# A two-layer block on one core: PV of a slot moved behind both its pairs of scores and of maxima, and the first batch's routing and expert tiles moved behind the first scores

## The reference

```python
x = L0_attn_x                                  # (4, 1024, 128) f32
xn = layernorm(x)
x = x + attn0(xn) + moe(xn)                    # layer 0
xn = layernorm(x)
x = x + attn1(xn) + fp4_ffn(xn)                # layer 1
```

## Time and profile before

| | us |
|---|---|
| median of 3 runs | 1758.02 |
| lowest and highest | 1752.01, 1764.23 |
| the profiled execution | 1775.41 |
| its span, first to last instruction | 1773.3 |
| PE, DVE, ACT, POOL busy | 1532.3, 1350.8, 1156.3, 580.5 |

### The profile page before, as it was taken

How to read it: one execution, slowest core, us unless ns; L and a number is a source line. 1 busy time by engine, 2 the same in 40 slices (tenths; PEclk the granted TensorE clock), 3 DMA queues, 4 the chain that set the end, 5 groups by cost and what they waited for, 6 DMA issues and landing times.

```text
span 1773.3 us, 35212 instructions
## 1 busy us (share of the span) xinstructions
PE 1532.3 (86%) x10813; PEld 643.4 (36%) x10813; DVE 1350.8 (76%) x3482; ACT 1156.3 (65%) x2716; POOL 580.5 (33%) x530
## 2 busy tenths in 40 slices
PE   3389969888999999778999999688999978989996
PEld 1233423333334444223333454233444424334332
DVE  6698858759998677659898866577888867888881
ACT  2067758747888566447887755455888864766665
POOL 3302120111454233241544414311141464553530
PEclk8599989979999899869999989888999987999999
DMA  7423622211612113321711112512353200310000
GB/s 228 110 83 95 163 60 69 63 42 42 179 46 58 31 47 120 89 72 44 188 45 34 57 31 77 164 44 63 96 163 102 62 26 2 101 44 2 14 2 13
DMA packets 162918, 131.84 MB, mean 74 GB/s; under 512 B 30825, under 2 KB 130098, under 8 KB 162738
## 3 DMA queue, kind: packets, MB, share of 16 engines
q1 hardware_dynamic: 158642, 121.19, 25.1%
q0 software_dynamic: 4096, 8.40, 1.6%
HBM read 88.50 MB, written 40.50 MB: 73 GB/s over the span
## 4 chain that ended last, share of the span: by engine, by line
PE 58%; DVE 20%; issue 7%; ACT 6%; another core or an unknown queue 4%; POOL 4%; SPq 1%; DMA 1%; DVEq 0%; ACTq 0%; POOLq 0%
PE ring L493 38%; PE pO L493 16%; DVE mparts L1108 10%; ACT PR L771 4%; PE ring L496 4%; DVE junk L1112 1%; DVE xn L1175 1%; POOL rows_in L695 1%; DVE hs L1398 1%; DVE xr L1288 1%; DVE hs L1397 1%; DVE stats L1158 1%; ACT hid L834 1%; POOL rstd L665 1%
## 5 line engine op out<-in xcount | busy, mean ns | idle before, releaser
L771 ACT ACTIVATE PR<-ring 128x512 f32<-128x512 f32 (+3 forms) x1792 | 882.9, 557 | 351.8 <-PE ring L493 292.9
L1108 DVE TENSOR_REDUCE mparts<-ring 128x1 f32<-128x512 f32 x1280 | 811.0, 683 | 211.0 <-PE ring L493 152.9
L493 PE MATMUL pO<-PR,VX 128*9 128x512 f32 (+3 forms) x3584 | 449.0, 575 | 7.6 <-ACT PR L771 6.9
L493 PE MATMUL ring<-KX,QX 48*128 48x512 bf16 (+3 forms) x1792 | 341.4, 376 | 93.1 <-ACT PR L771 60.6
L493 PE MATMUL ring<-QX,KX 50*128 50x512 bf16 (+3 forms) x1792 | 339.6, 375 | 59.4 <-DVE mparts L1108 35.6
L493 PEld LDWEIGHTS ring<-QX,KX 50*128 50x128 bf16 x1792 | 89.7, 93 | 519.2 <-DVE mparts L1108 244.4
L1112 DVE CUSTOM_DVE_ANT_0 junk<-ring,diag 128x384 bf16<-128x384 f32 (+3 forms) x512 | 227.8, 487 | 65.3 <-PE ring L493 55.2
L721 POOL TENSOR_SCALAR bq<-bq 128x352 f32<-128x352 f32 (+1 forms) x40 | 47.1, 1177 | 449.9 <-ACT bq L871 439.2
L493 PEld LDWEIGHTS ring<-KX,QX 48*128 48x128 bf16 x1792 | 96.3, 95 | 187.6 <-issue 77.1
L834 ACT ACTIVATE hid<-ring,b1r 128x128 f32<-128x128 f32 x368 | 105.2, 369 | 52.6 <-PE ring L493 47.4
L710 POOL DMA_INDIRECT ra<-rows_out,at x64 | 61.2, 956 | 234.4 <-DMA rows_out<-yb 141.6
(11 more groups left out here) (156 smaller groups left out, 1507.6 us busy)
## 6 DMA issues: line engine op xcount, KB each, us to landing
scratch<-parts SPq DMA_DIRECT2D x96, 256.0 KB, 3.7
w1r<-in_w SPq DMA_DIRECT2D x92, 256.0 KB
w2r<-in_w SPq DMA_DIRECT2D x92, 256.0 KB
QX<-scratch SPq DMA_DIRECT2D x128, 96.0 KB, 3.2
KX<-scratch SPq DMA_DIRECT2D x64, 192.0 KB, 3.8
xg<-rows_in SPq DMA_DIRECT2D x92, 64.0 KB
rows_out<-yb SPq DMA_DIRECT2D x92, 64.0 KB
QX<-mT SPq DMA_DIRECT2D x256, 2.0 KB
```

Of the source, the lines that this page charges most:

```text
L493: return nc.tensor.matmul(dst, lhsT, rhs, start=start, stop=stop, **kw)
L771: nc.scalar.activation(PR[:, n % 2, HALF * j + off:HALF * j + HALF], ring[plan.bank("E", k)][:, off:HALF], ACT.Exp, scale=SCALE).then_inc( ...
L1108: v.tensor_reduce(dst, src[:, 0:w], axis=X, op=ALU.max).then_inc(s_mr, 1)
```

## The change

It has five parts.

1. PE's order in a slot: first scores, first maxima, second scores, second maxima, then PV, then the pieces. ACT's four exponentials of a step stand together, and the copy of `pO` and the `hi` and `mid` copies follow them.
2. The first batch's gate logits, routing, scatters and tiles go behind the first scores: `lg` at slot 40, the scatters in slots 50 to 57, the tiles from slot 60 to 111 (before: 9, 19 to 26, and 29 to 102). The preparation of batch 1 moves from slots 42 to 61 to slots 59 to 70. The gathers of batch 0 move from slots 104 to 111 to slots 113 to 120. The turned fp4 weights (`wT`) go from slots 15 to 17 to 33 to 35.
3. Preparations may put three pieces in a slot (`most`).
4. The first four projection halves have four pairs of buffers, two of them lent by `hid` and `oT`, and their remainder on DVE is one step later in the slot. ACT waits for their readers before it writes `oT` and `hid` for the first time.
5. POOL clears the second operand set after the first four `lo` parts in place of after the first `rstd`, and the first loads wait for five clears in place of seven.

```diff
@@ -71,13 +71,17 @@
-                done = self.finish(p)
-                self.tiles(p)
+                self.finish(p)
+                if p:
+                    self.tiles(p)
...
-                    self.prepare(p + 1, self.start[p] + (2 if p else 4), self.projected[p - 1] + 1 if p else 0)
+                    self.prepare(p + 1, self.start[p] + 2 if p else self.gated[p] + T + 2,
+                                 self.projected[p - 1] + 1 if p else 0)
+                    if p == 0:
+                        self.tiles(p)
@@ -96,8 +100,8 @@
-    def put(self, i, event):
-        while len(self.slot(i)["xs"]) >= 2:
+    def put(self, i, event, most=2):
+        while len(self.slot(i)["xs"]) >= most:
@@ -146,7 +150,7 @@
-        to = {0: self.start[1] + 2, 1: self.start[3] - 4, 2: self.start[5] - 4, 3: self.start[6] - 8}[b]
+        to = {0: self.start[1] + 6, 1: self.start[3] - 4, 2: self.start[5] - 4, 3: self.start[6] - 8}[b]
@@ -171,6 +175,7 @@
+        at = max(at, self.start[0] - 6)
@@ -184,22 +189,22 @@
-            i = self.put(i + 1, ("xT", p, h))
+            i = self.put(i + 1, ("xT", p, h), 3)
...
-                    i = self.put(i + 1, ("pj", p, q, h, "a"))
-                    i = self.put(i, ("pj", p, q, h, "b"))
+                    i = self.put(i + 1, ("pj", p, q, h, "a"), 3)
+                    i = self.put(i, ("pj", p, q, h, "b"), 3)
...
-                        self.slot(i + 1)["small"][0].append(("rem", p, q, h))
+                        self.slot(i + 1)["small"][3].append(("rem", p, q, h))
...
-                    i = self.put(i + 1, ("pj", p, q, h, ""))
+                    i = self.put(i + 1, ("pj", p, q, h, ""), 3)
@@ -207,7 +212,8 @@
-            j = self.put(i + 1, ("lg", p))
...
+            j = self.put(i + 1 if p else self.start[0] + 2, ("lg", p))
@@ -517,6 +523,14 @@
+        def sums(n):
...
+            return hid[n % 2][:, :] if n in (2, 3) else ra[:, n % 2, :]
...
+        def left(n):
...
+            return oT[n % 2][:, :] if n in (2, 3) else rb[:, n % 2, :]
@@ -562,7 +576,7 @@
                                 sp.wait_ge(s_scr[q], 96 * (p + 1))
-                                sp.wait_ge(s_pre, 7)
+                                sp.wait_ge(s_pre, 7 if p else 5)
                                 if p >= 2:
@@ -663,25 +677,25 @@
-                            if p == 0:
-                                clear(1)
...
-                            nc.gpsimd.tensor_tensor(ra[:, n % 2, :], ra[:, n % 2, :], rb[:, n % 2, :],
+                            nc.gpsimd.tensor_tensor(sums(n), sums(n), left(n),
...
-                            nc.gpsimd.tensor_tensor(rb[:, n % 2, :], ra[:, n % 2, :], parts[:, q, 0, half],
+                            nc.gpsimd.tensor_tensor(left(n), sums(n), parts[:, q, 0, half],
...
-                            nc.gpsimd.tensor_tensor(parts[:, q, 2, half], rb[:, n % 2, :], parts[:, q, 1, half],
+                            nc.gpsimd.tensor_tensor(parts[:, q, 2, half], left(n), parts[:, q, 1, half],
...
+                            if lows == 4:
+                                clear(1)
@@ -750,11 +764,11 @@
-                def exps(s, js):
+                def exps(s):
...
-                    if js[0] == 0 and plan.steps[s["step"]] == 0:
+                    if plan.steps[s["step"]] == 0:
...
@@ -773,10 +787,13 @@
-                    exps(s, (0, 1))
+                    exps(s)
...
+                        if k == 0:
...
+                            act.wait_ge(s_lo, 4)
@@ -788,11 +805,10 @@
-                            copy(parts[:, q, 0, half], ra[:, n % 2, :]).then_inc(s_hi, 1)
+                            copy(parts[:, q, 0, half], sums(n)).then_inc(s_hi, 1)
...
-                            copy(parts[:, q, 1, half], rb[:, n % 2, :]).then_inc(s_mid, 1)
-                    exps(s, (2, 3))
+                            copy(parts[:, q, 1, half], left(n)).then_inc(s_mid, 1)
@@ -808,8 +824,8 @@
-                            if p == 0:
-                                act.wait_ge(s_pre, 7)
+                            if p < 2:
+                                act.wait_ge(s_pre, (5, 7)[p])
@@ -828,6 +844,9 @@
+                            if N == 0:
...
+                                act.wait_ge(s_rem, 4)
...
@@ -927,8 +946,9 @@
-                    scores(s, 0)
-                    maxima(s, 0)
+                    for pair in range(2):
+                        scores(s, pair)
+                        maxima(s, pair)
@@ -948,8 +968,6 @@
-                    scores(s, 1)
-                    maxima(s, 1)
@@ -1198,7 +1216,7 @@
-                            dve.wait_ge(s_pre, 7)
+                            dve.wait_ge(s_pre, 3)
...
@@ -1356,15 +1374,15 @@
-                            if n >= 2:
+                            if n >= 4:
...
-                                ins = v.tensor_tensor(ra[:, n % 2, :], src[:, :], rc[:, half], ALU.mult)
+                                ins = v.tensor_tensor(sums(n), src[:, :], rc[:, half], ALU.mult)
...
-                                ins = v.tensor_tensor(rb[:, n % 2, :], src[:, :], rs[:, half], ALU.mult)
+                                ins = v.tensor_tensor(left(n), src[:, :], rs[:, half], ALU.mult)
...
-                                ins = v.tensor_tensor(rb[:, n % 2, :], src[:, :], parts[:, q, 0, half], ALU.subtract)
+                                ins = v.tensor_tensor(left(n), src[:, :], parts[:, q, 0, half], ALU.subtract)
```

More of the change, by code:

```diff
@@ L767, in exps @@
                         act.wait_ge(s_pv, n - 1)
-                    for j in js:
+                    for j in range(G):
                         k = 4 * n + j
@@ L862, in _ @@
                             act.wait_ge(s_rem, plan.parts0[p, q, h] + 1)
-                            copy(parts[:, q, 1, HALF * h:HALF * h + HALF], rb[:, n % 2, :]).then_inc(s_mid, 1)
+                            copy(parts[:, q, 1, HALF * h:HALF * h + HALF], left(n)).then_inc(s_mid, 1)
                         if e[0] == "gates":
@@ L1298, in small_step @@
                         dve.wait_ge(s_hi, n + 1)
-                        v.tensor_tensor(rb[:, n % 2, :], ra[:, n % 2, :], parts[:, q, 0, HALF * h:HALF * h + HALF],
+                        v.tensor_tensor(left(n), sums(n), parts[:, q, 0, HALF * h:HALF * h + HALF],
                                         ALU.subtract).then_inc(s_rem, 1)
@@ L1410, in _ @@
                         if e[0] == "pj" and e[1] == 0 and e[4] == "b":
-                            v.tensor_tensor(ra[:, n % 2, :], ra[:, n % 2, :], rb[:, n % 2, :], ALU.add).then_inc(s_sum, 1)
+                            v.tensor_tensor(sums(n), sums(n), left(n), ALU.add).then_inc(s_sum, 1)
                     for e in s["small"][3]:
```

## The result

The changed kernel takes **1896.36 us** (median of 4 runs, 1890.74 to 1907.09) against 1755.01 us before: ratio **1.080**, 95% interval 1.073 to 1.087. The forecast was 1828 us with a range up to 1885. The direction was right, the size was half of what came: 141 us and not 70. The profiled execution took 1907.1 us, its span is 1905.4 us.

A forecast was written before the change was run, and what follows sets the result against it. PE, busiest at 86%, was taken to lose time to waits between engines, none near full. Terms 47 + 20 - 26 + 16 + 6 + 7 = +70 us on 1758.0 gave 1828 us; likeliest case 1783 to 1885, whole range 1735 to 1885.

The forecast's parts named there:

- the wait of the second maxima: Each full slot on PE: they wait 0.53 us for the exponential of their slot's first score; 187 us over 352 slots.
- What it gives back at the first pairs: First maxima on PE no longer wait for exponentials of the slot before's second scores: 95 us gained, between 65 and 185.
- The order within a slot: PV moved behind the second maxima on PE: 187 - 95 - 35 - 10 = +47 us, with no wait at second scores.
- The turns: PV and piece become neighbours on PE, saving one bf16/fp32 turn in some 390 attention slots: 35 us gained.
- The hidden layer: A tile's four activations on ACT delay the next slot's exponentials by 0.65 us: at most 60 us, taken as +20.
- The start: Before the first exponential: routing leaves the DVE chain, so it comes at 74 us instead of 100.28: -26 us.
- the clear of the second operand set: On GpSimd it moves behind the four parts, its readers coming a hundred microseconds later: no cost.
- The middle: Work moved beside attention costs time: scatters of batch 0 +16 us, routing on DVE +6, three more tiles +7.
- The scatters' price of 16 us: The 16 scatters of batch 0 beside attention idle engines: +16 us, with nothing at one end and 21 at the other.
- overfull slots: Rival: three pieces with two hidden layers hold ACT 2.3 us; 20 places at 2 us, upper ends, 1895 us; chance 0.03.
- faster: Rival: at least half of the new 0.53 us falls into slots DVE or ACT paces anyway: 1724 us; chance 0.21.
- The scatters are free: Rival: batch 0's scatters meet no tile transfers in the new plan and cost nothing: 1812 us; chance 0.12.

The follow-up runs named there:

- the order alone: The kernel before with only part 1 of the change (PV behind both pairs, four exponentials together): ratio 1.080, run again with a trace 1.073.
- the whole change: The changed kernel, unedited, run once more beside the others of the second group: 1902.03 us, ratio 1.080 to before.
- the order undone: The changed kernel with the slot's order of before on PE and ACT, all else kept: ratio 1.003, run again on another chip 1.009.
- all scatters paced: Scatters held to slots: all four batches in the changed kernel with the slot's old order, ratio 0.982; batches 1 to 3 in the kernel before, 0.983.
- the traced pair: The kernel before, unedited, and before with part 1 of the change only, traced on one chip: 1755.12 and 1898.64 us, ratio 1.073.

## Why the prediction was wrong

**The bound, and the wait of the second maxima: right.** 1.22 us from the slot's start was forecast, 1.23 measured; the wait 0.53 against 0.57 us (the median of the full slots without a hidden layer ahead); the sum ahead of the second maxima +197 against +199 us in the order alone. A run of its own supports it: about 0.38 us off the first exponential (0.60 to 0.23 us) gave 73 us here and 15 before.

**What it gives back at the first pairs: right there, but not kept.** -95 forecast, -99 measured. The prediction says "this wait goes" and asks for no pair behind the first ones; part of it came back ahead of the second scores.

**"The order within a slot": the step that failed.** It said that PE waits ahead of the second maxima "in each slot, with nothing that could run", and counted the cover of PV for this pair alone. It put the wait of the **second scores** at nothing. Their banks were last filled with the second maxima or a piece of the slot before, which DVE, and for some pieces ACT, reads late. Before, they were due only behind PV (259.79 against a slot's start of 257.58); now they are due 0.45 us after the start (308.29 to 308.74). That is 87 us in the order alone and 116 us in the whole change. 49 of the 87 are in slots after two pieces, where PV no longer stands between piece and scores. In the other slots it still lies between the second maxima and these scores; there DVE reads later, because the maxima come closer together, and the first pairs no longer hold the scores back. That split is read from the distances of two traces, no run parts it. The run with PV one place further down than before shows that the second scores can become the wait: 3.1% slower than before, 2.8% slower than with the order undone.

**The turns: right.** -35 forecast, -37 measured in the order alone. PV takes 0.97 us up to a bf16 pair (258.82 to 259.79) and the same up to a piece (310.50 to 311.47 above), so the piece's own 0.08 us goes.

**The hidden layer: right in kind, low in size.** The delay of 0.65 us is there in full, in 47 slots: 31 us where a third of 92 tiles, 20 us, was taken.

**The start: right by two errors that cancel.** Start 27.6 us against 26, first maxima at 45.22 against 45. But the clear of the second operand set, which the prediction moves "at nothing", was not free in either place. Before, it ran beside the norm, where DVE's eight steps took 6.21 us; now they take 2.14. And now it runs beside the weight steps, of which one takes 5.23 us where it took 0.20 (39.16 us, before). First the norm before; then, of now, the norm, the long weight step and the clear:

```profile
10.02 6.21 DVE L1175 TENSOR_SCALAR xn<-xr,mv,rstd 128x128 f32<-128x128 f32 x8 [1.79 <-POOL rstd L665]
```

```profile
10.06 2.14 DVE L1193 TENSOR_SCALAR xn<-xr,mv,rstd 128x128 f32<-128x128 f32 x8 [1.79 <-POOL rstd L679]
...
29.53 5.23 DVE L1140 TENSOR_SCALAR sc<-am 128x70 f32<-128x70 f32 x1
...
30.10 3.51 POOL L661 MEMSET KX<- 128x4096 f32 x1
33.55 1.17 POOL L662 MEMSET VX<- 128x1280 f32 x1
```

The long step ends at 34.76 us, the clear at 34.72. So 4.1 us were won and 5.0 lost, neither foreseen.

**The middle: right in kind.** What comes back: with the order undone the rest of the change is 5 us slower than before on one chip and 15 us on another, forecast +3. On the second chip the stop beside the scatters of batch 0 is in it. With all scatters paced there is neither gain nor loss from the new start (0.982 and 0.983): 27 us earlier at slot 38, level at slot 102. Within its groups PE takes 13 us more in the whole change than in the order alone (22 against 9), of which three tiles are 7. Most of the rest has a name: PE waits 5.6 us for `b1r<-in_b` in the whole change, and 0.5 in the order alone. With the order undone it waits 13.2 us for it on the first group's chip and 14.4 on the third's, 13.4 with the scatters paced; before, never. So the denser plan pays for late loads as well, which the prediction has not; no run changes those loads alone. The scatters' price of 16 us was near for the first chip (12.41 us of ACT), and too high for those on which nothing stops.

**The sum.** For the order 67 us was forecast and 144 came in the traced pair, 128 by the ratio and 133 by the medians; the second scores are 87 of it, and all other rows together are right within 10 us. Start and middle add 5 to 15 us where 3 was forecast. None of the rivals had this mechanism, and the upper end of 1885 us stood on larger values of terms that were known. By these it is not even 1885: hidden layers at 60 and scatters at 21 add 40 and 5 us to 1828, which is 1873, and with 40 us for overfull slots 1913, not 1895. The rival "faster" is refuted: it needed an idle time of under 0.36 us a slot on average, and 199 us over 352 slots are 0.57. Of the signs given, the slots came as forecast in the order alone, 2.53 us in the median without a piece (forecast 2.5) and 3.62 with a tile's first layer (3.6). "The scatters are free" depends on the chip.

## What to carry to other kernels

Before moving a long piece of work within an in-order stream, list **every** instruction that stands behind it and would wait without it, not only the one whose wait is nearest: here PV covered banks that ACT frees and banks that DVE frees, in slots that fill eight times what has seven banks. Then ask of each wait that the move takes away whether the next instruction only inherits it. Of the three places tried the one ahead of both pairs is the best; behind the second scores PV already cost 3%, behind both pairs 7 to 8%. An earlier start is worth only what the middle can take without waiting, which was nothing here, since the work that left the idle start went into slots that were full.

## What was not expected of the hardware

Beside 16 indirect DMAs, issued 1.26 us apart, PE, DVE and ACT stand together for 3 to 13.5 us with no wait that the trace names, on the chips where before took 1755 to 1766 us, and not on the two where it took 1672 and 1674 us. Eight unbroken gathers do the same for up to 6 us. Scatters spaced over the slots, as those of batch 1, stop nothing, which made a kernel 1.7% faster than before on a chip of the first kind; where gathers closed the pauses, 5.8 us of stop remained. No record names what the engines wait for.

A clear of 4.6 to 4.7 us on GpSimd held a step of 70 columns on DVE for its whole length: 5.23 us in place of 0.20. It is so in all nine traces with the plan of the change, on chips of both kinds, and in none of the nine with the plan of before, where the same clear stands beside the norm and its steps take 6.21 us in place of 2.14. No run moves the clear alone; what ties the two is that the held step ends when the clear does, in both places (14.63 against 14.55 us at the norm, 34.76 against 34.72 at the weight step).
